# Issuing the token loads of the layer norm from the ScalarE queue in place of the GpSimd queue, in a transformer layer on eight cores

## The reference

```python
xn  = ln(x)                                   # x: (16, 2048, 1024)
qkv = xn @ Wqkv.T + bqkv                      # 16 heads of 64
s   = mask + q k^T / 8                        # over the 16 positions of one batch column
att = softmax(s) v ; a = att @ Wproj.T + bproj
h   = silu(xn @ w1.T * w1_s) * (xn @ w2.T * w2_s)     # 4096 wide
h   = gelu(h @ h1.T * h1_s)
h   = gelu(h @ h2.T * h2_s)
out = x + a + h @ w3.T * w3_s
```

## Time and profile before

| | us |
|---|---|
| time before, median of 2 runs | 6707.66 |
| lowest and highest of these | 6630.03 and 6785.29 |
| the profiled execution, its own time | 5822.24 |
| its span on the slowest core (core 1) | 5820.7 |
| spans of the 8 cores | 5795.5 to 5820.7 |

### The profile page before, as it was taken

How to read it: one execution, slowest core, us unless ns; L and a number is a source line. 1 busy time by engine, 2 the same in 40 slices (tenths; PEclk the granted TensorE clock), 3 DMA queues, 4 the chain that set the end, 5 groups by cost and what they waited for, 6 DMA issues and landing times.

```text
span 5820.7 us, 71560 instructions; the slowest of 8 cores (5795.5 to 5820.7 us)
## 1 busy us (share of the span) xinstructions
PE 5540.5 (95%) x26368; PEld 2497.3 (43%) x26368; DVE 1127.6 (19%) x3360; ACT 1165.8 (20%) x2177; POOL 146.9 (3%) x287
## 2 busy tenths in 40 slices
PE   5787788999999999999999999999999999999999
PEld 2333333444444444444444444444444444444444
DVE  2140001240023300242002510124002330024100
ACT  0241000241103310142001510024100331014100
POOL 1000000000000000000000000000000000000000
PEclk9898899999999999999999999999999999999999
DMA  8999998434444443434434444444434444344443
GB/s 179 212 215 223 220 217 222 170 143 165 158 155 151 154 165 151 167 136 155 173 130 174 149 170 155 157 152 148 171 149 170 145 146 173 145 159 145 159 158 117
DMA packets 88161, 961.00 MB, mean 165 GB/s; under 512 B 8512, under 2 KB 8592, under 8 KB 29072
## 3 DMA queue, kind: packets, MB, share of 16 engines
q0 software_dynamic: 38208, 470.92, 28.7%
q1 hardware_dynamic: 32976, 451.95, 20.8%
q10 hardware_dynamic: 16640, 33.56, 1.7%
HBM read 939.61 MB, written 117.44 MB: 182 GB/s over the span
## 4 chain that ended last, share of the span: by engine, by line
PE 83%; DMA 15%; issue 1%; DVE 0%; POOL 0%; ACT 0%; DVEq 0%; POOLq 0%; ACTq 0%; SPq 0%
PE PSF L234 76%; DMA wbuf<-h 6%; PE PSF L230 5%; DMA h_bf<-wbuf 4%; DMA wbuf<-w 3%; PE PSF L388 1%; DMA wbuf<-wqkv 1%; DMA wbuf<-wproj 1%; DMA w_bf<-wbuf 0%; DMA wqkv_bf<-wbuf 0%; PE PSB L472 0%; PE PSF L384 0%; PE PSB L474 0%; PE PSB L313 0%; DVE Ao L512 0%
## 5 line engine op out<-in xcount | busy, mean ns | idle before, releaser
L234 PE MATMUL PSF<-Ar,wbuf 128*128 128x512 bf16 x9920 | 2217.1, 382 | 79.8 <-DMA wbuf<-h 51.0
L234 PE MATMUL PSF<-Br,wbuf 128*128 128x512 bf16 x7936 | 1784.8, 384 | 65.2 <-DMA wbuf<-h 65.2
L234 PEld LDWEIGHTS PSF<-Ar,wbuf 128*128 128x128 bf16 x9920 | 962.5, 98 | 1248.8 <-issue 120.8
L234 PEld LDWEIGHTS PSF<-Br,wbuf 128*128 128x128 bf16 x7936 | 782.8, 99 | 1028.1 <-issue 112.9
L234 PE MATMUL PSF<-xn_f,wbuf 128*128 128x512 bf16 x4480 | 1085.4, 383 | 54.0 <-DMA wbuf<-w 48.1
L234 PEld LDWEIGHTS PSF<-xn_f,wbuf 128*128 128x128 bf16 x4480 | 441.1, 99 | 594.4 <-issue 75.4
L699 ACT ACTIVATE Ar<-PSF,v_h2s 128x512 bf16<-128x512 f32 x256 | 175.9, 687 | 1816.1 <-PE PSF L230 1816.1
L720 DVE SCALAR_TENSOR_TENSOR sum_f<-PSF,v_w3s,sum_f 128x512 f32<-128x512 f32 x64 | 48.1, 751 | 2286.2 <-PE PSF L230 2286.2
L570 DVE SCALAR_TENSOR_TENSOR Ar<-PSF,v_w2s,t 128x512 bf16<-128x512 f32 x256 | 192.2, 751 | 753.4 <-PE PSF L230 753.4
L550 ACT ACTIVATE t<-PSF,v_w1s 128x512 bf16<-128x512 f32 x256 | 175.2, 687 | 683.3 <-PE PSF L230 683.2
L636 ACT ACTIVATE Br<-PSF,v_h1s 128x512 bf16<-128x512 f32 x256 | 175.9, 687 | 658.3 <-PE PSF L230 656.5
(11 more groups left out here) (68 smaller groups left out, 1679.0 us busy)
## 6 DMA issues: line engine op xcount, KB each, us to landing
wbuf<-h_bf POOLq DMA_DIRECT2D x112, 2048.0 KB, 8.3
wbuf<-h_bf SPq DMA_DIRECT2D x112, 2048.0 KB, 9.1
wbuf<-w_bf POOLq DMA_DIRECT2D x42, 2048.0 KB, 8.1
wbuf<-w_bf SPq DMA_DIRECT2D x42, 2048.0 KB, 8.0
wbuf<-h POOLq DMA_DIRECT2D x32, 2048.0 KB, 33.3
h_bf<-wbuf SPq DMA_DIRECT2D x32, 2048.0 KB, 25.3
wbuf<-w POOLq DMA_DIRECT2D x12, 2048.0 KB, 30.8
w_bf<-wbuf SPq DMA_DIRECT2D x12, 2048.0 KB, 22.3
```

The costliest lines, as they stand in the source:

```text
L234: return lambda e: e.matmul(out=out, lhsT=lhsT, rhs=rhs, start=start, stop=stop, tile_position=tile_position)
```

## The change

The load of `xt` is put on ScalarE's program in place of GpSimd's. Nothing else changes.

```diff
@@ phase_L_pre_group @@
                 a = xls[slot].inc(16)
-                E.add("gpsimd", WM(("xt", slot)),
+                E.add("scalar", WM(("xt", slot)),
                       lambda e, a=a, t=t, g=g, slot=slot: a(e.dma_start(
                           out=xt[:, slot, :],
                           in_=x_in[(t * T + g * P):(t * T + (g + 1) * P), :])))
```

## The result

| | us |
|---|---|
| changed kernel, median of 11 runs | 5981.24 (5844.6 to 6314.53) |
| kernel before, median of 10 runs | 6391.46 (5815.76 to 6830.45) |
| ratio changed to before, 95% interval | 1.0046 (1.003 to 1.0062) |
| profiled execution of the changed kernel | 5842.24, its span 5840.5 (core 5) |

The ratio uses only the executions in which all cores had a granted clock of about 0.98, and there the two kernels take about 5847 and 5822 us; in the others the cores of one die or of both had a lower one (0.81 to 0.96), and the two runs of before from which the prediction started, 14 and 17% above 5822 us, are too long for the first sort. So the change costs 0.46% of 5822, or 27 us (17 to 36). A difference of this size is within the 2% band: "same", and slightly slower.

The account below looks back on a forecast made before the run. Tile 0 was taken as bound by its weight loads, casts and copies, the rest by TensorE. Terms 12 + 12 + 3 = +27 us, added to the 6707.7 us median, gave 6735 us, range 6620 to 6860.

Parts of the forecast that it names:

- I carry the sum over unscaled: Whole kernel: +27 us added unchanged to the 6707.7 us median of the runs shown, giving 6735 us.
- The sum: Whole kernel: all terms together, +27 us on the profiled execution's 5822.2 us, giving 5849, +0.5%.
- 12 + 12 + 3: Terms in us for h1 of tiles 1 to 6, h1 of tile 0, and the start.
- Part 1: h1 of tiles 1 to 6, 24 places: TensorE waits for Gelus behind the `xt` load, +12 us.
- free part: h1: landing time of `xt` that costs TensorE nothing, 7.5 us in tiles 1 to 6, 14.8 in tile 0.
- 2 x 0.5: h1, each of tiles 1 to 6: two places with 8 us landings cost 1 us, rounded up to 2.
- Part 2: h1 of tile 0, four places: 21 us landings stall TensorE 25 us, about half comes back, +12 us.
- Part 3: Program start: phase Q begins at 53.2 in place of 39.9 us, weights earlier, net +3 us.
- Part 4: GpSimd's program: loses 32 DMAs and their waits, but isn't late with any, so nothing comes free.
- Rival 2: All `xt` places: landing stays 9.7 us, +73 us, 6781 us; chance 0.16.
- Rival 1: h1: ScalarE's queue is starved, landings 12.3 us, 38 in tile 0; +219 us, 6927 us; chance 0.12.
- Rival 3: Start and tile 0: early weights win, stalls hidden, start gives 10 us; -10 us, 6698 us; chance 0.17.

Follow-up runs that it names:

- e3_h1_later: Against the kernel before, only the `xt` loads in h1 of tiles 1 to 6 moved to ScalarE's queue; ratio 1.0024 (1.0009 to 1.0038).
- e2_h1_tile0: Against the kernel before, only the four `xt` loads in h1 of tile 0 moved to ScalarE's queue; ratio 1.0001 (0.9988 to 1.0015).

## Why the prediction was right or wrong

- **The time of 6735 us and its range (6620 to 6860) were wrong**: 5981 us is far below. The step that failed is the last one, "I carry the sum over unscaled". The text noted that the two runs lay 15% above the profiled execution and that the profile doesn't say why, and then widened the range only by their spread of 77 us. Of ten runs of before, four took 5816 to 5823 us, the level of the profiled execution (5822), and the changed kernel took 5845 to 5850 us in five of its eleven. The profiled execution should have been a case of its own for the level, and the range should have reached down to 5820.
- **The sum, +27 us or +0.5%, was right**: 27 us (17 to 36). So were the class (within 2%) and the side of zero. Luck has a part in so close an agreement: the terms were 12 + 12 + 3, and the parts alone measure 14 + 0 + 5.
- **Part 1, +12 us for tiles 1 to 6**: measured +13.2. The free part of 7.5 us held (7.6 at the place shown). The landings were forecast as 8 us at two places per tile and 5 at two others; they are 8.8 to 11 at one place and 3 to 5 at three. The total came right by luck: I took `gi` 20 and 26 as alike, and they differ by who issues the weights beside them. "2 x 0.5", doubled, stands for what is one stall of 1.2 to 3.4 us. What a stall brings with it was forecast as another 1 us on 1; it is 0.4 us on 1.8.
- **Part 2, +12 us for h1 of tile 0**: alone it measured 0 (-7 to +9), within the bounds given (0 to 60) and smaller than the value taken. Two errors work against each other in it. The landings of up to 26 us were longer than the 21 of the packet count, and the free part, forecast as 14.8 us at every place, was 11.0, 7.6 and 7.5 us at the three that stalled (core 5: 26.0 - 15.0, 25.6 - 18.05, 20.8 - 13.3); so the stalls sum to 46 us in place of 25. And the DMA engines gave back nearly all of it, where I had said half.
- **Part 3, +3 us for the start**: +5 us (-2 to +12), or +7 by the mean over the cores. Q at 53.2 was forecast, 53.97 came. The third and fourth `xt` landed in 14.7 and 11.5 us, where 11.8 was forecast from a load with as many packets. The Trainium skill (DMA: Bandwidth & Descriptors, "Queues, rings and completion order") has the DMA engines take turns between queues by the packet. The trace agrees once both queues have packets: 62 of the weights against 64 of `xt` from 2003 to 2006 us.
- **Part 4, nothing from GpSimd**: no run gained from its shorter program; e3_h1_later, which takes 24 of the loads from it, costs 13 us in the very tiles.
- **Rival 2 (9.7 us everywhere, +73 us)** fell: 36 of 48 landings are under 5 us. The Trainium skill (same page, "Issuing engines are not separate DMA queues") says that DMAs of different engines interleave on the same DMA engines and that the choice saves only issue time. That is not the whole story here: the same load beside 2 MB of weights took 4.7 or 9.4 us according to the engine that issued the neighbour. **Rival 1 (starved queue)** has its mechanism in tile 0 only. **Rival 3 (early weights win)** is not seen in the change, where the loads stand in series with Exp; without this series the start gains 6 to 8 us, near the 10 that the rival gave it.

## What to carry to other kernels

A load that is issued by a compute engine directly ahead of the work that needs it turns its whole landing time into a wait of that engine (10.75 us here for a landing of 9.4), and of everything behind it. Count the time to the moment at which the bottleneck needs what is queued behind (here 7.5 us): below it the move is free, above it each microsecond counts, once per place. Issued some steps earlier, the same load on the same queue cost nothing here in tiles 1 to 6. And take the level of a time from the execution that was profiled when it disagrees with the runs, or give both.

## What was not expected of the hardware

- A load of 512 KB on ScalarE's queue lands in 3.1 to 4.3 us when all weight loads of 2 MB come from GpSimd's queue (core 1), and in the changed kernel in 8.8 to 11.0 beside one from SyncE's. Beside GpSimd's its packets pass first; beside SyncE's the weights come first, and then the two take turns packet by packet, 4 KB against 16.
- Stalls of 56 us in the stretch that is bound by DMA cost 0 us (-7 to +9) in the end, although the group of matmuls behind each of the three long ones took 8.2 to 9.1 us in place of 6.85 (e2_h1_tile0, core 0).
- A stretch of 4132 us of this kernel repeats within 0.7 us over the cores, the chips and the variants that don't stall in it (4131.7 to 4132.4), while the 980 us ahead of it vary by 25 us from core to core, and their mean, by the estimate above, by up to 15 us from chip to chip.
